# The first layer's attention: sixteen periods written out, or seven and a loop

## The reference

```python
x = x + conv_attn(group_norm(x))          # 3x3 conv to 192 channels beside attention to 64
# attention: 8 heads of 8 channels over 1024 tokens of an image
logits  = einsum('bnid,bnjd->bnij', q, k) + rel_w + rel_h   # relative logits by row and column
weights = softmax(logits, axis=-1)
attn    = einsum('bnij,bnjd->bnid', weights, v) @ attn_w + attn_b
# layer 1: t = to_tokens(x)
t = t + self_attention(layer_norm(t))     # one head of 128 over 1024 tokens
t = t + experts(layer_norm(t))            # 2 of 8 experts for each image, 256 -> 512 -> 256
```

## Time and profile before

| | us |
|---|---|
| median of 3 runs | 2419.05 (2417.93 to 2420.2) |
| the profiled execution, its time | 2417.93 |
| its span, first to last instruction | 2416.2 |
| stretch of the 16 periods in the span | 630 to 1434 |
| PE busy in the span | 2175.0 (90%) |
| ACT busy | 1214.4 (50%) |
| DVE busy | 1342.2 (56%) |

### The profile page before, as it was taken

How to read it: one execution, slowest core, us unless ns; L and a number is a source line. 1 busy time by engine, 2 the same in 40 slices (tenths; PEclk the granted TensorE clock), 3 DMA queues, 4 the chain that set the end, 5 groups by cost and what they waited for, 6 DMA issues and landing times. The chain is left out here.

```text
span 2416.2 us, 30025 instructions
## 1 busy us (share of the span) xinstructions
PE 2175.0 (90%) x10534; PEld 1508.0 (62%) x10534; DVE 1342.2 (56%) x2054; ACT 1214.4 (50%) x2160; POOL 329.9 (14%) x274
## 2 busy tenths in 40 slices
PE   4999999947899999999999964988888893999997
PEld 3777888846455545544555422777777772888886
DVE  6232333235777777777777602566565642565665
ACT  1121222122477777777677752555555552565664
POOL 1000000010032112121122202222221100000000
PEclk9999999955799999999999996999999996999999
DMA  2322233396766777667776214233332115334531
GB/s 73 90 76 65 66 135 118 118 191 214 169 120 106 114 105 121 109 106 115 106 119 108 71 41 121 72 101 101 100 100 95 41 44 206 125 127 167 197 122 62
DMA packets 150444, 268.02 MB, mean 111 GB/s; under 512 B 31808, under 2 KB 94016, under 8 KB 146240
## 3 DMA queue, kind: packets, MB, share of 16 engines
q1 hardware_dynamic: 141344, 240.76, 41.6%
q0 software_dynamic: 7680, 25.17, 3.2%
q10 hardware_dynamic: 1312, 0.67, 0.1%
HBM read 156.62 MB, written 107.25 MB: 109 GB/s over the span
## 5 line engine op out<-in xcount | busy, mean ns | idle before, releaser
L647 DVE TENSOR_REDUCE a_nmax<-a_sm 128x1 f32<-128x1024 f32 x512 | 604.0, 1220 | 192.3 <-PE a_sm L667 192.3
L903 ACT ACTIVATE p_shared<-a_st 128x512 f32<-128x512 f32 x1024 | 556.8, 597 | 234.9 <-PE a_st L928 233.3
L943 PE MATMUL a_pv<-p_shared,a_va 128*32 128x512 f32 x2048 | 272.5, 604 | 0.9 <-ACT p_shared L903 0.9
L928 PE MATMUL a_st<-a_qf,a_kf 121*128 121x512 f32 x704 | 253.8, 438 | 10.1 <-ACT p_shared L903 8.0
L667 PE MATMUL a_sm<-a_kf,a_qf 120*128 120x512 f32 x704 | 217.8, 429 | 39.9 <-DMA a_kf<-kq_d 24.7
L928 PEld LDWEIGHTS a_st<-a_qf,a_kf 121*128 121x128 f32 x704 | 119.0, 188 | 208.5 <-ACT p_shared L903 198.0
L1818 PE MATMUL x_h_ps<-x_v_hi,x_w 128*128 128x512 f32 x512 | 180.8, 395 | 25.1 <-DVE x_v_lo L1759 25.1
L667 PEld LDWEIGHTS a_sm<-a_kf,a_qf 120*128 120x128 f32 x704 | 135.9, 203 | 77.0 <-issue 24.9
L1832 PE MATMUL x_y_ps<-x_h_hi,x_w 128*128 128x512 f32 x512 | 178.0, 389 | 0.0
L1769 DVE SCALAR_TENSOR_TENSOR x_h_lo<-x_hid,x_wts,x_h_hi 128x512 fp32r<-128x512 f32 x128 | 96.1, 750 | 138.2 <-ACT x_h_hi L1740 138.2
L1736 ACT ACTIVATE x_hid<-x_h_ps,x_b 128x512 f32<-128x512 f32 x128 | 88.4, 691 | 130.3 <-PE x_h_ps L1818 125.4
(11 more groups left out here) (250 smaller groups left out, 3669.8 us busy)
## 6 DMA issues: line engine op xcount, KB each, us to landing
x_w<-w_d SPq DMA_DIRECT2D x32, 1024.0 KB, 8.5
rel_d<-p_shared SPq DMA_DIRECT2D x12, 2048.0 KB, 12.2
a_qf<-rel_d SPq DMA_DIRECT2D x22, 512.0 KB
a_qf<-rel_d SPq DMA_DIRECT2D x44, 256.0 KB
c_xtok<-in_x SPq DMA_DIRECT2D x8, 1024.0 KB, 5.9
va_d<-c_va SPq DMA_DIRECT2D x16, 512.0 KB, 4.7
rel_d<-a_hl SPq DMA_DIRECT2D x4, 2048.0 KB, 20.3
a_va<-va_d SPq DMA_DIRECT2D x32, 256.0 KB
```

The source lines that it names most:

```text
L647: nc.vector.tensor_reduce(nmax[:, h, t:t + 1], sm[k % 2][:], axis=AX.X, op=ALU.max, negate=True).then_inc(sm_read, 1)
L903: nc.scalar.activation(probs[:, t % 2, h, half * HALF:(half + 1) * HALF], st[half][:], ACT.Exp).then_inc(exp_done, 1)
L928: nc.tensor.matmul(st[half][:], kf[j][0:ROW_M + 1, h, t * P:(t + 1) * P], qf[j][0:ROW_M + 1, h, 2 * t // TT, half * HALF:(half + 1) * HALF ...
L943: m = nc.tensor.matmul(pv[32 * h:32 * h + 32, cols], va[j][:, t, h, :], probs[:, t % 2, h, cols], start=t == 0, stop=t == TT - 1, skip_gro ...
```

## The change

`all_groups` now calls period 0 with plain numbers, puts periods 1 to 12 into a loop of four passes of three periods, and calls periods 13 to 15 with plain numbers again. With NG = 16 and BUFS = 3, `steps` is 4 and the loop counts n = 1, 4, 7, 10. The buffers of each period in the body are those that it had before. POOL's list is the same as before. Lines behind line 605 move down by five, so line 903 of before is line 908 of after, and so on.

```diff
         def all_groups(eng, period):
 
-            for n in range(NG):
+            steps = (NG - 3) // BUFS
+            period(0, 0, True, True)
+            with eng.Fori(1, (steps - 1) * BUFS + 2, BUFS) as n:
+                for i in range(BUFS):
+                    period(n + i, (1 + i) % BUFS, True, True)
+            for n in range(1 + steps * BUFS, NG):
                 period(n, n % BUFS, n < NG - 1, n + 2 < NG)
```

## The result

The changed kernel takes 2439.61 us (median of 4 runs, 2436.12 to 2440.03), the kernel before 2419.28 us beside it. The ratio is 1.0084, 95% interval 1.0069 to 1.0098: slower by 20.3 us. The direction was forecast, the size was not (2427.5, range to 2436).

What follows compares the result with a forecast made beforehand. PE and ACT waiting for each other set the pace of the changed periods. 2417.9 + 0.5 + 0.0 + 6.0 + 2.0 = 2426.4; the runs' median is 1.1 above the profiled one, giving 2427.5 us, range 2417.5 to 2436.

Steps and rivals of the forecast that it cites:

- Part 1: Attention loop's steady state: added register operations on PE and ACT stay mostly hidden, 0.5 us in all, ends 0 and 8.6.
- the ring: Attention periods: PE's loads and products and ACT's exponentials wait for each other, 3.10 us a turn, sixteen times a period.
- Part 2: Three jumps back of the attention loop: PE or ACT waits for its dropped first piece, 2.0 us each, 6.0 in all.
- the part under the queued loads: At each attention jump, 0.9 us of the 2.9 us fetch lies under PE's four queued weight loads.
- The piece ahead is one too many: PE has room for 8 instruction pieces; the attention body touches 8, so the piece fetched behind it does not fit.
- Part 3: Self-attention: DVE's moved loop body touches 4 pieces instead of 3, stops at two jumps, 1.0 us each, 2.0 in all.
- All pieces are held: Rival: the engines hold the whole attention body, only part 1 stays, 2419.6 us, no change; chance 0.30.
- Register waits in the ring: Rival: 0.09 us exposed 96 times, 2435.6 us, up to 2441 with stops in series; chance 0.13 including stops in series.
- Less fetching helps: Rival: instruction pieces no longer fetched had held up transfers or jumps between stages; 2418 us or faster; faster: chance 0.05.
- two-page window: Skill's rule: a taken branch outside the current two pages forces a fetch; the trace spoke against it, in self-attention's loop.
- room of 2048 instructions: Skill's figure for PE, estimated as 8 pieces: self-attention's 6 fit, the new attention body with the piece ahead does not.

Runs made afterwards that it cites:

- DVE-only run: Attention loop of periods 1 to 12 on DVE alone, PE, ACT and SP written out, against the kernel before: 2424.82 us, ratio 1.0027.
- the pauses: Kernel before with 8, 12, 16 and three times 28 unused semaphore increments on PE at the head of six periods: 2440.26 us, ratio 1.0082.
- PE's loop alone: Kernel before with the loop of periods 1 to 12 on PE alone, SP, ACT and DVE written out, no hint: 2431.09 us, ratio 1.0055.
- eight-piece expert body: Kernel before, PE's expert-stage loop lengthened by 28 unused semaphore increments a unit, to 1792 instructions: 2584.2 us, single run.
- the placed body: Changed kernel with branch hint on all engines, DVE's self-attention loop body placed to touch three instruction pieces instead of four: 2423.59 us, ratio 1.002.
- the same loop on PE with the hint: Kernel before with the loop on PE alone plus a hint that its jump goes back to the head: 2417.52 us, ratio 0.9993.
- the runs at seven and eight pieces: Kernel before, PE's expert-stage loop lengthened by 20 or 28 unused semaphore increments a unit: 2479.7 and 2584.2 us, single runs.
- the run with the placed head: Loop on PE alone against the kernel before, no hint, its head to be placed on the start of a piece: 2432.41 us, ratio 1.006.
- the run with the hint on all engines: Changed kernel plus a branch hint at the attention loop's head on SP, ACT, DVE and PE, against the kernel before: 2426.3 us, ratio 1.0036.
- the run with ACT's short loop and the hint: Changed kernel, hint on all engines, DVE's self-attention body placed, ACT looping once a period instead of once in three: 2435.8 us, ratio 1.0069.

## Why the prediction was wrong in size

- **Part 1, 0.5 us: right.** The nine undisturbed periods of the loop are 0.5 us longer in sum, and no register wait shows in the ring. The 3.0 us of the DVE-only run are not explained, so this is right for the changed kernel and not for every mix of loops.
- **Part 2, stops of 2.0 us each: this step failed, in two ways.** That they come, where, on which engines, and on which queue was right, and so was the part under the queued loads (0.9 us). The stop was mis-sized: a missed jump takes 3.5 to 3.9 us where 2.9 was taken from the landing times of the earlier trace rows, so PE's matmuls stand for 3.0, 3.0 and 2.7 us, 8.6 in all instead of 6.0. And the sum had no term for what follows a stop: the clock at half for 6.8, 6.8 and 3.4 us. At the prices of the pauses that is 2.6 + 2.6 + about 1.8 = 7.0 us, more than the whole step. For PE's loop alone this working closes: stops of 2.6, 3.5 and 3.0 us and the clock at half for 3.4, 6.8 and 3.4 us make 9.0 + 6.2 = 15.2 of the 15.3 us in its periods. In the changed kernel 1.3 of the 16.9 us are left, which no run isolates; ACT's own stop is over before PE's is at all three jumps. The earlier trace rows had slices of low clock in stages where PE waits; that a new wait brings one was there to be asked.
- **The reason given for the stop was half right.** "The piece ahead is one too many" holds, but it was applied as a count of pieces touched. By it the eight-piece expert body would have stopped, and it ran free. The body of the changed kernel ends at 0.78 of its last piece (by my count), so here the forecast of a stop came true by that place, which is in part luck.
- **Part 3, 2.0 us: right in kind, half in size.** DVE stands for 3.0 us at each of two jumps, 2.5 us longer than before, and that costs 3.9 us where 2.0 was taken; the loop on DVE alone brings the stops, and the placed body takes them away. Less of a stop is taken back in that stage than was assumed.
- **Rivals.** "All pieces are held" is refuted for the changed kernel, and true of the same loop on PE with the hint. "Register waits in the ring" gave 2435.6 to 2441 and would have matched the time by the wrong mechanism: periods within a pass are 50.1 to 50.3 us. "Less fetching helps": q8 brought more, 75 packets instead of 65.

The two-page window of the Trainium skill ("Runtime: NRT & Kernel Launch", section on instruction fetch mechanics) is contradicted for PE also by the runs at seven and eight pieces: jumps of 0.21 to 0.22 us and no packet on q8. Its room of 2048 instructions for PE, eight pieces, agrees with the runs here: bodies that touch eight are held, unless a ninth is fetched before the jump.

## What to carry to other kernels

In this kernel a jump back was nearly free where the whole body was still on the engine, and cost microseconds where it was not. So count the pieces per engine, see where in the last one the body ends, and look for instruction packets on the queues in the second pass. Price a missed jump on PE as the stop plus the slow clock behind it (here about 3 us and 1.7 to 2.6 us), and look for the same effect in later loops whose place in the list moves. The remedy here was different for each engine (hint for PE, shorter body for ACT, placement for DVE), and all of it together only bought back the time of the code written out.

## What the runs showed of the hardware

- Where PE's matmuls stood for 2.6 to 3.5 us, the clock was at 1.2 GHz for 3.4 or 6.8 us; which of the two, the length of the stop does not say (3.4 behind 3.0 us and 6.8 behind 2.9 in the run with the placed head). One of 8.1 us went with 10.2 us. One of 1.7 us in the run with the hint on all engines went with 3.4; ones of 0.8 and 1.4 us in the run with six pauses left the clock alone.
- 60 increments of a semaphore follow each other on PE at 0.15 us each.
- A missed jump takes 3.4 to 4.3 us on PE; on ACT the instruction behind it comes 2.1 to 3.0 us later (0.2 to 0.3 where the body is held), on DVE 2.8 to 3.0 (0.3 to 0.4).
- In the run with ACT's short loop and the hint, with the data queue at 103.8% of the transfer engines' time, the instruction packet came 11.6 us after ACT's last instruction. That it had to wait for data is a reading, not shown.
